# Where the edge network's second product of layer 2 is made: in the cluster pass of layer 1, or per node tile inside the MLP

## The chip, the cores and the metric

The kernel runs on one core of one Trainium2 chip. The metric is the device time of one launch in microseconds (us), here the median of three runs. A change of this kernel within about 0.2% (6.5 us) can't be told from no change.

## The reference, cut to what matters

Four graph layers run one after the other on 3,750 nodes with 256 features and 63,750 edges. Each adds its result to x. The change touches only how layer 2's edge term is made:

```python
# layer 1 (cluster layer), cut
logits = gcn_conv(h, W)          # 256 -> 10, summed over neighbours with a normalised adjacency
x = x + h + softmax(logits) @ cluster_emb
...
# layer 2, cut
e   = relu(ea @ ee_w1 + ee_b1) @ ee_w2 + ee_b2      # per edge: 64 -> 256 -> 256
agg = segment_sum(h[src] + e, dst)
h   = (1 + eps) * h + agg
h   = relu(ln(h @ w1 + b1)); h = relu(ln(h @ w2 + b2)); y = h @ w3 + b3    # the MLP, 256 -> 1024 -> 1024 -> 256
x   = x + relu(ln(h_in + y))
```

The sum over edges and the product with `ee_w2` can be exchanged, so the kernel sums the hidden rows `relu(ea @ ee_w1 + ee_b1)` per node during layer 0's edge loop, and multiplies by `ee_w2` once per node. With deg the number of edges of a node, the edge term is `HS^T @ ee_w2 + deg * ee_b2`.

## The kernel before, in words

There are NT = 30 node tiles of P = 128 nodes, taken as NJ = 15 pairs in the MLP. Five engines run programs of their own, written out by hand in the order in which they run, and synchronised by counting semaphores; there is no scheduler. `SUMS` holds five rows of 3,880 node columns: `HS` is rows 3 and 4 (the hidden sums, 256 features by nodes), `AG` rows 1 and 2, `DEG` row 0. `EW2` is `ee_w2`. `PS` is PSUM, eight banks of 512 float32.

The stages that matter here, in order:

- The **cluster pass** of layer 1 (TensorE L1072 to L1108). The adjacency matrix lies in DRAM as bfloat16 (`a_d`), and SyncE loads it tile by tile (`adjacency`) in column groups of 1,024: groups 0 to 3 have 30 tiles of 256 KB each, group 4 has 30 tiles of 166 columns. There are NR = 7 buffers; a tile can be loaded only when the tile seven places before it was used (`a_used`). For each wide tile TensorE makes two matmuls (L1088, 30 x 512). In groups 0 and 1 it also spreads the degree row to all partitions in eight matmuls (`spread_counts`, L1068, one after every seventh tile), each copied out by ScalarE (L689). VectorE writes 24 one-hot blocks (`first_one_hot`, L1589, from L1714) and then, in `cluster_sums`, copies each group's sums out of PSUM (L1671, L1673) and sends `d_free`. TensorE's group g from 2 on waits for `d_free` of group g-2.
- Softmax and the turned rows of layer 2. VectorE then adds `DEG * ee_b2` to `AG` in two instructions (L1763), and `neighbours` adds the neighbour sums.
- The **MLP** (TensorE from L1138, loop `dense_pair`). A pair is tiles i = 0 and 1. The order in TensorE's program for pair j is: dense1(1,j), dense2(0,j) first half, turn_hidden(1,j,0), dense2(0,j) second half and dense2(1,j) first half, turn_hidden(0,j,1), edge_part(0,j+1), dense2(1,j) second half, dense1(0,j+1), dense3(0,j), turn_hidden(1,j,1), edge_part(1,j+1), turn_hidden(0,j+1,0), dense3(1,j). All dense products are L1153, the turns L822, edge_part L1145. `edge_part` makes four products of 128 x 128 into the tile's PSUM bank, and VectorE's `dense_in` (L1783) adds them to `AG` and writes `HIN`, the input of dense1.
- VectorE per layer and tile: `hidden_stats` (L1790 to L1795, then the two scalars L1777 and L1778); per tile `dense_out` (from L1803). It writes the tile's output out of the PSUM banks that turn_hidden(i,j+1,0) needs next: that turn waits for `m_out`. ScalarE: `hidden_norm` (L723, L725) and `hidden_relu` (L736), of which dense3 waits for the last of eight.

A float32 matmul is shown in the trace as two records. So edge_part's four products are eight records, dense3's eight are sixteen.

## Time and profile before

| | us |
|---|---|
| median of 3 runs | 3268.11 |
| lowest, highest | 3263.8, 3269.29 |
| profiled execution: span on the page | 3494.0 |
| its own device time | not given, so the span stands for it |

| stretch of the profiled execution, us from its start | what runs |
|---|---|
| to 1777 | layer 0 and its edge loop, scatters of the adjacency |
| 1817 to 1927 | cluster pass |
| 1927 to 2330 | softmax, neighbour sums of layer 2 |
| 2330 to 3087 | MLP |
| 3087 to 3494 | layer 3 |

The profiled execution is 226 us longer than the median of the timed runs. Which of its stages are stretched the page can't tell; the change works in two stages and its effect is counted as a difference there, in us, and put on the median.

How to read it: "busy" is the time in which an engine executes; the number in brackets at a row's end is how long the engine sat idle before that row, and what it waited for. Matmuls are pipelined, so the distance from one row's start to the next one's is what a row costs, not its duration.

### The profile page before, as it was taken

The numbers are of one execution on the slowest core, as the hardware profiler recorded it, in microseconds if no ns is written. First come the engines' busy times: TensorE is split into PE (matmuls) and PEld (weight loads), VectorE is DVE, ScalarE is ACT, GpSimd is POOL, SyncE is SP. The second block draws the span as 40 slices with busy tenths as digits, with TensorE's granted clock in tenths as the row PEclk, the third lists the DMA queues.
The fourth block names the chain that finished last, engine by engine and source line by source line (L and its number), as shares of the span: only waits on it lengthen the run. The fifth ranks groups of instructions, "written<-read, shape, count | busy, mean of one in ns | idle before, by whom it ended". The sixth has DMA issues, their size and how long they took to land.

```text
span 3494.0 us, 48240 instructions
## 1 busy us (share of the span) xinstructions
PE 2934.6 (84%) x15020; PEld 1947.6 (56%) x15084; DVE 1869.1 (53%) x5320; ACT 1260.7 (36%) x3665; POOL 1013.3 (29%) x1048
## 2 busy tenths in 40 slices
PE   2799936888888888889268799989999999999998
PEld 2444416777777777778142444445555555545545
DVE  6578745666666665556250543334555555532334
ACT  1122235666666666668020220004444444420000
POOL 2144465666666666665710000000000000000000
PEclk6699968898999899999559699999999999999999
DMA  8966643222222222221128243330000000022232
GB/s 250 363 180 194 183 125 86 70 73 74 71 74 71 73 74 72 74 66 28 31 71 301 82 119 103 101 118 6 3 6 6 6 3 6 23 76 79 78 101 80
DMA packets 245032, 314.35 MB, mean 90 GB/s; under 512 B 121467, under 2 KB 168484, under 8 KB 240740
## 3 DMA queue, kind: packets, MB, share of 16 engines
q1 hardware_dynamic: 191412, 175.79, 17.8%
q0 software_dynamic: 49104, 104.11, 10.2%
q10 hardware_dynamic: 4320, 31.95, 2.3%
q8 instruction: 109, 1.79, 0.2%
q14 instruction: 87, 0.71, 0.1%
HBM read 234.14 MB, written 77.59 MB: 89 GB/s over the span
## 4 chain that ended last, share of the span: by engine, by line
PE 57%; DVE 15%; issue 11%; ACT 7%; another core or an unknown queue 4%; DVEq 3%; DMA 3%; SPq 0%; ACTq 0%
PE PS L1153 15%; PE PS L998 14%; PE PS L964 7%; PE PS L939 5%; PE PS L977 5%; PE PS L822 4%; ACT BG L653 3%; DMA BG<-a_d 3%; DVE BG L1703 2%; DVEq L1582 2%; DVE OHB L1430 1%; ACT SL L736 1%; DVE AL L1790 1%; DVE SUMS L1411 1%
## 5 line engine op out<-in xcount | busy, mean ns | idle before, releaser
L1567 DVE TENSOR_TENSOR SUMS<-SUMS,PS 128x640 f32 x500 | 409.2, 818 | 374.2 <-PE PS L939 220.7
L532 POOL DMA_INDIRECT BG<-feat_d,IDXST x500 | 485.9, 972 | 337.9 <-PE PS L939 157.4
L523 POOL DMA_INDIRECT a_d<-VAL,IDXS x499 | 492.3, 987 | 314.3 <-DVE VAL L1424 133.2
L1153 PE MATMUL PS<-BG,SL 128*128 128x512 f32 (+1 forms) x1440 | 539.1, 530 | 12.0 <-ACT SL L736 12.0
L653 ACT ACTIVATE BG<-BG,SL 128x64 f32<-128x64 f32 x2000 | 513.4, 336 | 0.0
L1153 PEld LDWEIGHTS PS<-BG,SL 128*128 128x128 f32 x1440 | 277.0, 195 | 251.7 <-issue 222.4
L564 POOL MEMSET BG<- 128x7680 f32 x1 | 6.5, 6501 | 1327.3 <-DVE MV L1834 1327.3
L964 PE MATMUL PS<-W1A,X 65*128 65x256 f32 x1000 | 295.2, 421 | 81.8 <-ACT X L627 60.4
L939 PE MATMUL PS<-OHB,BG 128*128 128x128 f32 x2000 | 357.2, 305 | 0.2
L977 PE MATMUL PS<-OHB,X 128*128 128x128 f32 x2000 | 337.5, 295 | 23.1 <-issue 22.6
L977 PEld LDWEIGHTS PS<-OHB,X 128*128 128x128 f32 x2000 | 306.7, 208 | 40.0 <-issue 25.1
L939 PEld LDWEIGHTS PS<-OHB,BG 128*128 128x128 f32 x2000 | 287.3, 207 | 1.8
L822 PE MATMUL PS<-IDENT,X 128*128 128x128 f32 (+3 forms) x700 | 167.6, 282 | 103.2 <-issue 80.3
L964 PEld LDWEIGHTS PS<-W1A,X 65*128 65x128 f32 x1000 | 184.8, 206 | 118.2 <-ACT X L627 74.3
L634 ACT ACTIVATE X<-PS 128x512 f32<-128x512 f32 x250 | 148.7, 595 | 264.2 <-PE PS L964 128.5
L871 PE MATMUL PS<-SUMS,BG 128*128 128x512 f32 x480 | 241.9, 635 | 0.0
L723 ACT ACTIVATE SM<-SM,EPSC 128x1 f32<-128x1 f32 x60 | 17.7, 294 | 539.9 <-DVE SM L1795 539.9
L998 PE MATMUL PS<-AL,BG 128*128 128x512 bf16 (+1 forms) x906 | 192.2, 368 | 4.5 <-DVE SUMS L1758 3.0
L998 PE MATMUL PS<-AL,SUMS 128*128 128x512 bf16 (+1 forms) x893 | 187.3, 364 | 5.2 <-DVE X L1906 3.0
L736 ACT ACTIVATE SL<-PS,COL 128x128 f32<-128x128 f32 x480 | 173.7, 475 | 26.0 <-PE PS L822 25.9
L1703 DVE TENSOR_TENSOR SUMS<-SUMS,OHB 128x2 f32 x499 | 81.6, 163 | 159.1 <-issue 93.0
L599 ACT ACTIVATE SUMS<-PS 128x512 f32<-128x512 f32 x120 | 71.6, 597 | 259.9 <-PE PS L871 219.2
(298 smaller groups left out, 4093.0 us busy)
## 6 DMA issues: line engine op xcount, KB each, us to landing
BG<-a_d SPq DMA_DIRECT2D x171, 256.0 KB, 4.2
AL<-a_d SPq DMA_DIRECT2D x137, 256.0 KB, 2.6
a_d<-BG POOLq DMA_DIRECT2D x30, 1088.0 KB, 40.2
feat_d<-SUMS ACTq DMA_DIRECT2D x30, 1040.0 KB
BG<-rel_d SPq DMA_DIRECT2D x100, 160.0 KB
X<-in_edge_attr_dram SPq DMA_DIRECT2D x124, 128.0 KB
SUMS<-a_d SPq DMA_DIRECT2D x52, 256.0 KB, 2.6
SL<-key_d SPq DMA_DIRECT2D x50, 192.0 KB
```

The lines of the kernel that those rows point to most:

```text
L523: pool.indirect_dma_start(a_d.rearrange("n (w o) -> (n w) o", o=1), bass.IndirectOffsetOnAxis(ap=IDXS[:, t:t + 1], axis=0), VAL[:, t:t + 1 ...
L532: pool.indirect_dma_start(RING[:, t // NB % 3, t % NB, :], None, feat_d.rearrange("n (r d) -> (n r) d", r=R), bass.IndirectOffsetOnAxis(ap ...
L653: last = act.activation(m, m, ACT.Copy, scale=EXT[:, b % 2, k, 1 + q:2 + q])
L736: last = act.activation(H1T[:, i, c, :], PS[:, 4 + 2 * i + c // 4, (c % 4) * P:(c % 4 + 1) * P], ACT.Relu, scale=COL8[:, 2 * l, c:c + 1], ...
L822: return pe.transpose(out_ap, in_ap, IDENT[0:k, 0:k])
L871: last = pe.matmul(PS[:, 4 + q, :], HT[:, c, t * P:(t + 1) * P], WALL[:, c, q * 512:(q + 1) * 512], start=(c == 0), stop=(c == 1))
L939: last = pe.matmul(at[:, (c + 1) * P:(c + 2) * P], RING[:, b % 3, k, c * P:(c + 1) * P], OH[:, k % 10, :], start=True, stop=True)
L964: last = pe.matmul(EDGE_HIDDEN[:, k * D:(k + 1) * D], EAT[v % 2][:, 2 * q + k, :], W1A[:, :], start=True, stop=True)
L977: pe.matmul(SUM_AT[n % 3][:, (3 + c) * P:(4 + c) * P], HM[v % 2][:, k, c * P:(c + 1) * P], OH[:, n % 10, :], start=True, stop=True)
L998: last = pe.matmul(PS[:, 4 * (g % 2) + 2 * c + o // 512, 0:m], lhs(t, part)[:, c * P:(c + 1) * P], rhs[:, o:o + m], start=(t == 0 and part ...
L1153: last = pe.matmul(PS[:, to + q, 0:width], lhs[:, i, c, :], w[:, c, q * width:(q + 1) * width], start=(c == 0), stop=(c == kc - 1))
L1567: add = tt(a, a, SUM_AT[n % 3].rearrange("p (a n) -> p a n", a=5), ALU.add)
```

## The change

The `ee_w2` products of all 30 tiles are made in groups 0 and 1 of the cluster pass. After the matmuls of an adjacency tile TensorE makes one `edge_part`, for the first time after tile 4 of group 0 and then 30 times up to tile 27 of group 1, into PSUM banks 6 and 7 in turn (waiting for `ee_home` of the tile two before). VectorE's new `edge_home` adds `DEG * ee_b2` and writes the result over `HS`, in two instructions per tile; it stands ahead of each one-hot block. VectorE starts `cluster_sums` only after all 30. `spread_counts` goes to banks 4 and 5 and stands after every third tile of group 0. Later one addition `AG += HS` takes the place of the two of L1763. In the MLP `edge_part` and its semaphores are gone, and `dense_in` is a copy of `AG` to `HIN`.

```diff
@@ ScalarE
-                act.activation(DEG[:, 512 * c:512 * c + n], PS[:, 4 + c % 4, 0:n], ACT.Copy).then_inc(s("deg_sb"), 1)
+                act.activation(DEG[:, 512 * c:512 * c + n], PS[:, 4 + c % 2, 0:n], ACT.Copy).then_inc(s("deg_sb"), 1)
@@ TensorE, cluster pass
-                if c >= 4:
-                    pe.wait_ge(s("deg_sb"), c - 3)
+                if c >= 2:
+                    pe.wait_ge(s("deg_sb"), c - 1)
...
+            def edge_part(e):
+
+                if e >= 2:
+                    pe.wait_ge(s("ee_home"), e - 1)
+                for f in range(2):
+                    for c in range(2):
+                        last = pe.matmul(PS[:, 6 + e % 2, f * P:(f + 1) * P], EW2[:, c, f * P:(f + 1) * P],
+                                         HS[:, c, e * P:(e + 1) * P], start=(c == 0), stop=(c == 1))
+                last.then_inc(s("ee_ps"), 1)
...
                 if g == 2:
                     pe.wait_ge(s("deg_sb"), 8)
+                    pe.wait_ge(s("ee_home"), NT)
...
-                    if g < 2 and t % 7 == 6:
-                        spread_counts(4 * g + t // 7)
+                    if g == 0 and t % 3 == 0 and t // 3 < 8:
+                        spread_counts(t // 3)
+                    if edges_home < NT and (g * NT + t - 4) * NT >= edges_home * 54:
+                        edge_part(edges_home)
+                        edges_home += 1
@@ TensorE, MLP
-            def edge_part(i, j):
-
-                for f in range(2):
-                    for c in range(2):
-                        last = pe.matmul(PS[:, 2 * i, f * P:(f + 1) * P], EW2[:, c, f * P:(f + 1) * P],
-                                         HS[:, c, bass.ds((2 * j + i) * P, P)], start=(c == 0), stop=(c == 1))
-                last.then_inc(s(f"m_ee{i}"), 1)
...
                 turn_hidden(0, j, 1)
-                if more:
-                    pe.wait_ge(s("m_var0"), 2 * j + 2)
-                    edge_part(0, j + 1)
                 dense2(1, j, 1)
...
                 if more:
-                    edge_part(1, j + 1)
                     turn_hidden(0, j + 1, 0)
                 dense3(1, j)
 
-            edge_part(0, 0)
-            edge_part(1, 0)
@@ VectorE
+            def edge_home(e):
+
+                dve.wait_ge(s("deg_sb"), e // 4 + 1)
+                dve.wait_ge(s("ee_ps"), e + 1)
+                for c in range(2):
+                    last = stt(out=HS[:, c, e * P:(e + 1) * P], in0=DEG[:, e * P:(e + 1) * P], scalar=B2C[:, c:c + 1],
+                               in1=PS[:, 6 + e % 2, c * P:(c + 1) * P], op0=ALU.mult, op1=ALU.add)
+                last.then_inc(s("ee_home"), 1)
...
-            for i in range(6 * LB):
-                last = first_one_hot(i // 6, i % 6)
-            step(last)
+            for e in range(NT):
+                edge_home(e)
+                if e < 6 * LB:
+                    last = first_one_hot(e // 6, e % 6)
+                if e == 6 * LB - 1:
+                    step(last)
+            dve.wait_ge(s("ee_home"), NT)
             cluster_sums()
...
-            for c in range(2):
-                step(stt(out=AG[:, c, 0:NPAD], in0=DEG[:, 0:NPAD], scalar=B2C[:, c:c + 1], in1=AG[:, c, 0:NPAD],
-                         op0=ALU.mult, op1=ALU.add))
+            step(tt(AG[:, :, 0:NPAD], AG[:, :, 0:NPAD], HS[:, :, 0:NPAD], ALU.add))
...
             def dense_in(i, j):
-                dve.wait_ge(s(f"m_ee{i}"), j + 1)
-                mine(dve, tt(HIN[:, i, :, :], AG[:, :, bass.ds((2 * j + i) * P, P)],
-                             PS[:, 2 * i, 0:D].rearrange("p (c n) -> p c n", c=2), ALU.add), f"m_hin{i}", j + 1)
+                mine(dve, cp(HIN[:, i, :, :], AG[:, :, bass.ds((2 * j + i) * P, P)]), f"m_hin{i}", j + 1)
```

TensorE in groups 0 and 1 of the cluster pass, before: L1088 is the adjacency product, L1068 the spread of the degrees. This is the start of group 0 and what follows it.

```order
4713 L1088 MATMUL PS<-BG 30x512 x14
4714 L1068 MATMUL PS<-SUMS,ONES 128x512
4715 L1088 MATMUL PS<-BG 30x512 x14
4716 L1068 MATMUL PS<-SUMS,ONES 128x512
4717 L1088 MATMUL PS<-BG 30x512 x14
```

The same place after, from tile 3 of group 0 on; L1099 is the adjacency product now, L1077 the four products of an edge_part.

```order
4716 L1068 MATMUL PS<-SUMS,ONES 128x512
4717 L1099 MATMUL PS<-BG 30x512 x2
4718 L1077 MATMUL PS<-SUMS,EW 128x128 x4
4719 L1099 MATMUL PS<-BG 30x512 x4
4720 L1068 MATMUL PS<-SUMS,ONES 128x512
4721 L1077 MATMUL PS<-SUMS,EW 128x128 x4
4722 L1099 MATMUL PS<-BG 30x512 x4
4723 L1077 MATMUL PS<-SUMS,EW 128x128 x4
```

Between two edge_parts stand one or two adjacency tiles (two or four matmuls) and nothing else but a spread.

TensorE in the MLP's loop, before, from the second turn (turn_hidden(0,j,1)) to the turn behind dense3(0,j):

```order
4850 L822 MATMUL PS<-IDENT,AL 128x128 x8
4851 L1145 ISA
4852 L1145 MATMUL PS<-SUMS,EW 128x128
4853 L1145 ISA
4854 L1145 MATMUL PS<-SUMS,EW 128x128 x3
4855 L1153 MATMUL PS<-BG,SL 128x512 x8
4856 L1158 REGISTER_ALU
4857 L1153 MATMUL PS<-BG,OHB 128x512 x4
4858 L1153 MATMUL PS<-BG,SL 128x256 x8
4859 L822 MATMUL PS<-IDENT,AL 128x128 x8
4860 L1145 ISA
```

and after, with the dense products at L1159, up to dense3(1,j):

```order
4905 L822 MATMUL PS<-IDENT,AL 128x128 x8
4906 L1159 MATMUL PS<-BG,SL 128x512 x8
4907 L1164 REGISTER_ALU
4908 L1159 MATMUL PS<-BG,OHB 128x512 x4
4909 L1159 MATMUL PS<-BG,SL 128x256 x8
4910 L822 MATMUL PS<-IDENT,AL 128x128 x8
4911 L1179 ISA
4912 L822 MATMUL PS<-IDENT,AL 128x128 x8
4913 L1159 MATMUL PS<-BG,SL 128x256 x8
```

The two turns at the end of a pair follow each other directly now. VectorE around the one-hot blocks (L1589), at the end of them and ahead of the first copy of `cluster_sums` (L1671 before, L1680 after), before and then after:

```order
2339 L1713 ISA
2340 L1589 SCALAR_TENSOR_TENSOR BG<-IOTA,QC,BG 125x640 x24
2341 L1671 COPY OHB<-PS 30x512
2342 L1673 COPY SUMS<-PS 30x512
```

```order
2386 L1670 SCALAR_TENSOR_TENSOR SUMS<-SUMS,COL,PS 128x128 x2
2387 L1589 SCALAR_TENSOR_TENSOR BG<-IOTA,QC,BG 125x640
2388 L1670 SCALAR_TENSOR_TENSOR SUMS<-SUMS,COL,PS 128x128 x12
2389 L1680 COPY OHB<-PS 30x512
2390 L1682 COPY SUMS<-PS 30x512
```

L1670 is edge_home; the copies of group 0's sums now stand behind the last of them.

## Rows read from the trace of the kernel before

**Rows 1.** The page: busy time of TensorE, and the chain by engine

```profile
PE 2934.6 (84%) x15020; PEld 1947.6 (56%) x15084; DVE 1869.1 (53%) x5320; ACT 1260.7 (36%) x3665; POOL 1013.3 (29%) x1048
PE 57%; DVE 15%; issue 11%; ACT 7%; another core or an unknown queue 4%; DVEq 3%; DMA 3%; SPq 0%; ACTq 0%
```

**Rows 2.** Busy time by stretch: groups 0, 1, 2 with 3

```profile
core 0: us, PE busy (x) PEld busy (x) DVE busy (x) ACT busy (x) POOL busy (x), PEclk, DMA share, GB/s
1817.20:1842.00 24.80, 22.25 (x68) 5.92 (x68) 18.91 (x24) 2.39 (x4) 0.00 (x0) 0.85 0.94 320
1842.00:1866.50 24.50, 21.16 (x74) 5.46 (x72) 1.79 (x3) 3.18 (x5) 0.00 (x0) 1.00 0.98 343
1866.50:1914.20 47.70, 38.61 (x254) 11.23 (x254) 3.65 (x9) 0.31 (x1) 0.00 (x0) 1.00 0.91 313
```

**Rows 3.** TensorE in order of time, groups 0 and 1: start us, duration us

```profile
1817.25 1.87 PE L1088 MATMUL PS<-BG 128*30 128x512 bf16 x4 [3.82 <-DMA BG<-a_d]
...
1825.45 3.19 PE L1088 MATMUL PS<-BG 128*30 128x512 bf16 x14
1828.57 1.12 PE L1068 MATMUL PS<-SUMS,ONES 1*128 1x512 f32 x2
1829.62 1.04 PE L1088 MATMUL PS<-BG 128*30 128x512 bf16 x4
...
1865.96 0.62 PE L822 MATMUL PS<-IDENT,OHB 30*125 30x30 f32 x4
```

**Rows 4.** VectorE in time there; then a tile of SUMS (ns min/median/max)

```profile
1816.92 19.19 DVE L1589 SCALAR_TENSOR_TENSOR BG<-IOTA,QC,BG 125x640 bf16<-125x640 f32 x24
1842.47 0.68 DVE L1671 COPY OHB<-PS 30x512 f32<-30x512 f32 x1 [6.36 <-PE PS L1088]
...
L1758 DVE TENSOR_SCALAR SUMS<-PS,COL x60: 399/402/410, 1981.2 to 2057.6; 128x128 f32<-128x128 f32 x60
```

**Rows 5.** TensorE in order of time, one pair of the MLP

```profile
2502.18 1.05 PE L822 MATMUL PS<-IDENT,AL 128*128 128x128 f32 x8
...
2517.68 1.06 PE L1145 MATMUL PS<-SUMS,EW 128*128 x8
2518.58 7.03 PE L1153 MATMUL PS<-BG,SL 128*128 128x512 f32 x16
2525.45 3.60 PE L1153 MATMUL PS<-BG,OHB 128*128 128x512 f32 x8
...
2533.21 1.06 PE L1145 MATMUL PS<-SUMS,EW 128*128 x8
2535.61 1.06 PE L822 MATMUL PS<-IDENT,AL 128*128 128x128 f32 x8 [1.35 <-DVE BG L1803]
2537.30 3.72 PE L1153 MATMUL PS<-BG,SL 128*128 128x256 f32 x16 [0.63 <-ACT SL L736]
...
2551.16 1.05 PE L822 MATMUL PS<-IDENT,AL 128*128 128x128 f32 x8
```

**Rows 6.** VectorE and ScalarE in order of time, the same pair

```profile
2525.65 1.23 DVE L1790 TENSOR_TENSOR AL<-PS,BG 128x1024 f32<-128x1024 f32 x1 [5.37 <-PE PS L1153]
...
2533.03 0.16 DVE L1778 SCALAR_TENSOR_TENSOR SM<-SM 128x1 f32<-128x1 f32 x1
2534.49 0.42 DVE L1783 TENSOR_TENSOR OHB<-SUMS,PS 128x256 f32<-128x256 f32 x1 [1.30 <-PE PS L1145]
...
2533.23 1.24 ACT L725 ACTIVATE AL<-AL,SM 128x1024 f32<-128x1024 f32 x1 [0.49 <-DVE SM L1778]
2534.38 2.88 ACT L736 ACTIVATE SL<-PS,COL 128x128 f32<-128x128 f32 x8
```

**Rows 7.** A dense3(1,j) at the lower clock: TensorE in time, and by stretch

```profile
2684.23 5.41 PE L1153 MATMUL PS<-BG,SL 128*128 128x256 f32 x16 [0.64 <-ACT SL L736]
...
2685.00:2687.50 2.50, 2.50 (x8) 1.96 (x7) 1.54 (x4) 2.15 (x7) 0.00 (x0) 0.50 0.00 0
```

**Rows 8.** TensorE in order of time, the first instructions of the MLP

```profile
2330.37 2.02 PE L1145 MATMUL PS<-SUMS,EW 128*128 128x128 f32 x16 [0.74 <-DVEq L1696]
2332.23 3.60 PE L1153 MATMUL PS<-BG,OHB 128*128 128x512 f32 x8
```

More of the change, by code:

```diff
@@ L1063, in spread_counts @@
             def spread_counts(c):
-                if c >= 4:
-                    pe.wait_ge(s("deg_sb"), c - 3)
+                if c >= 2:
+                    pe.wait_ge(s("deg_sb"), c - 1)
                 n = min(512, AW - 512 * c)
-                pe.matmul(PS[:, 4 + c % 4, 0:n], ONES[0:1, :], SUMS[0:1, 0, 512 * c:512 * c + n],
+                pe.matmul(PS[:, 4 + c % 2, 0:n], ONES[0:1, :], SUMS[0:1, 0, 512 * c:512 * c + n],
                           start=True, stop=True).then_inc(s("deg_ps"), 1)
+            def edge_part(e):
[6 more added lines that the diff above has]
+                last.then_inc(s("ee_ps"), 1)
             def cluster_turn(t):
@@ L1074, in _ @@
             pe.wait_ge(s("ys_ready"), 1)
-            turned = 0
+            turned = edges_home = 0
             for g, (c0, w) in enumerate(GROUPS):
```

## The prediction

> **What bounds the kernel now.** TensorE is busy for most of the span and heads the chain [rows 1], but a share says nothing of the two stages that the change touches, so I read each by itself: first the stretches, then the order of time on TensorE, then on the engines that it waits for.
>
> In the cluster pass the transfers set the pace. Their share is 0.94 and 0.98 in groups 0 and 1, at 320 and 343 GB/s [rows 2], and TensorE waits again and again for a tile of the adjacency. Its own need there is less than its busy time looks. Where it isn't waiting, 14 matmuls go from 1825.45 to 1828.57 [rows 3], 0.223 us each, so the 120 of both groups need 26.8 us. A spread takes 1.05 us (1828.57 to 1829.62), eight about 8.2. The first five us run at the lower clock (the granted mean of group 0 is 0.85 [rows 2], that is about 7 of 24.8 us at half of full speed, of which TensorE sat waiting for part), which costs about 2.5. Together 37.5 us. The two groups take 48.7 (1817.25 to 1865.96). So TensorE has some 11 us to spare, no more.
>
> In the MLP TensorE sets the pace, with two waits in each pair of tiles: 1.35 us ahead of turn_hidden(0,j+1,0), for VectorE's output addition L1803, and 0.63 ahead of dense3(1,j), for ScalarE's L736 [rows 5]. A pair takes 48.98 us (2502.18 to 2551.16), and there are 15.
>
> **The change part by part.** *Products added to the cluster pass.* An edge_part costs 0.90 us (2517.68 to 2518.58 [rows 5]) at the full clock. Thirty are 27.0 us; between matmuls of another shape a little more of a weight load may show, so I take 0.95, 28.5 us. 37.5 + 28.5 = 66.0 us of TensorE against 48.7 now: **17.3 us** later at the end of group 1, and TensorE has become the bound there. The bounds are 27.0 us with nothing lost between shapes (+15.8) and 31 (+19.8), if an edge_part costs 0.13 more or TensorE waits now and then for ee_home. VectorE keeps up, but only just: two instructions like L1758, 0.40 us each [rows 4] (the nearest row: 128x128, out of PSUM, with a pointer scalar), and a one-hot of 19.19 / 24 = 0.80 make 1.6 us per tile, against 1.8 adjacency tiles of 0.45 and one edge_part, 1.75 us, on TensorE. Two banks take up the jitter.
>
> *The added wait.* VectorE copies group 0's sums only after the last edge_home, and TensorE's group 2 waits for that copy. Behind edge_part 29 TensorE has two tiles left, 0.9 us. VectorE needs 0.8 for edge_home, 0.68 for L1671 [rows 4] and the same for L1673, and about 0.2 between them: 2.4. So TensorE stands 1.5 us: **+1.5**, nothing at best. Queued behind that wait is all of group 2, and SyncE's transfers behind it, since no buffer comes free.
>
> *What the slower groups give back.* While TensorE is the bound, transfers run ahead until all seven buffers are full. Groups 2 and 3 are still bound by transfers: 60 tiles in 47.7 us [rows 2], 0.795 each. They start with up to seven tiles in hand, worth at most 5.6 us; the transfers must start again behind the wait, which takes some 2 us of it away. I take **-4**, between -5.6 and -2. The cluster pass in all: 17.3 + 1.5 - 4 = **+14.8**, from 10 to 19.
>
> *Spread of the degrees.* The same eight matmuls, earlier; counted above. ScalarE copies each in time, three tiles before the bank is needed again. Zero.
>
> *The two additions L1763.* One addition of 7,680 elements in place of two of 3,840: the same VectorE work within a few tenths, and TensorE is in the neighbour sums meanwhile, which wait for nothing here. Zero; if the cover were gone, a few tenths.
>
> *Products taken out of the MLP.* 28 edge_parts of 0.90 us stand in 14 of the pairs, 25.2 us. Whether both of a pair count is to be read from the waits. edge_part(0,j+1), at 2517.68, stands ahead of dense2(1,j)'s second half with no wait near: it goes in full, 0.90 us. Everything after follows from the end of that dense2, T = 2525.45 [rows 5]. VectorE starts its statistics at T + 0.20 and works through two tiles' of them without a pause to L1778, done at T + 7.74 [rows 6]; ScalarE's L725 runs on from T + 7.78, and only then the eight L736 of tile 1, from T + 8.93 to T + 11.81; dense3(1,j) starts at T + 11.85 (2537.30). In none of this does edge_part(1,j+1) stand, which ran at T + 7.76 in TensorE's spare time. So it saves **nothing**: the wait grows. Turn_hidden(0,j+1,0) comes earlier, because dense_in (which waited 1.30 us for the products, 2534.49 [rows 6]) is a copy that starts at once: L1803 ends near T + 8.7 and not at T + 10.0. But dense3(1,j) still starts at T + 11.85. TensorE's waits in a pair become about 0.9 + 1.95 = 2.9 us in place of 1.98. From dense3(1,j) on the chain is the same as now. So 14 x 0.90 = **-12.6**. The first pair has its two products on the way from VectorE's last sum to dense1: 1.86 us (2330.37 to 2332.23 [rows 8]) become a copy of some 0.4 and its semaphores: **-1.2**. In all -13.8.
>
> *The clock.* In 5 of the 14 pairs the granted clock fell to 0.50, the lower level of 1.2 GHz, just after these two waits, and dense3(1,j) took 5.41 us in place of 3.72 [rows 7]: 1.7 us each, 8.5 us in all. What TensorE did before each fall was always the same 1.98 us of waits with eight transposes between. With 2.9 us of waits in the same place I expect more falls, 9 to 11 of 14, each at 1.5 us on average (part of some falls will lie in the waits): 15 us against 8.5, **+7**; bounds -2 (even fewer falls than now, three or four) and +12 (all 14). The Trainium skill ("TensorE: Matmul & The Clock Gate", "Why this matters for your kernels") puts the fall down to idle gaps between bursts that are longer than any wait in this loop; by it there would be no falls here, before or after. The trace disagrees: 5 falls with no wait above 1.35 us.
>
> Sum: 14.8 - 13.8 + 7 = **+8**, to 3268.1 + 8 = **3276 us**. On the profiled execution it would be 3494 + 8 = 3502. That one is 226 us longer than the median; nothing in the two stages shows a stretch, so I take the difference over as it is.
>
> **The rivals.** (A) The forecast, **3276** (3270 to 3284). Chance 0.48.
>
> (B) All as above, but the falls of the clock stay about as frequent, since they come and go with the phase of something that TensorE's program doesn't set: 9 of the 14 turns with the very same 1.98 us had none. (By the rule of the clock page cited above, waits of this size change nothing either, which is this case.) +1, **3269** (3265 to 3273). Chance 0.22.
>
> (C) The products hide under the transfers: TensorE waits for tiles in groups 0 and 1 and its weight loads (PEld) fill only 5.92 and 5.46 us of 24.8 and 24.5 [rows 2]. Even with all 27.0 us of the products added that is 38 of 49 us, below the stage's length. The cluster pass then costs at most 3 us: 3 - 13.8 + 7 = -4, **3264** (3258 to 3268). Against it: the streaming time of 0.223 us a matmul. It decides if the two groups end less than 5 us later. The Trainium skill ("Perfetto Trace Analysis", "Identifying the Most-Contended Engine") judges TensorE's room by just this share of weight loads, not by matmul busy time. Chance 0.10.
>
> (D) Both products of a pair are won, as a TensorE that waits only 2 us of 49 would suggest: 14.8 - 25.2 - 1.2, and with no waits added no more falls: -12, **3256**. It would need dense3(1,j) to start less than T + 11.85; the rows of VectorE and ScalarE leave no room for that. Chance 0.07.
>
> (E) The ending on the dear side: VectorE, not TensorE, paces the 30 edge_parts. If edge_home with its waits costs 1.1 us and not 0.8, a tile costs VectorE 1.9 to 2.0 us against 1.75, over the 24 that have a one-hot beside them: 4 to 6 us more, and TensorE's pauses may lower the clock there as well. 8 + 8, **3284** and above, to 3292. It decides once VectorE's step per tile is over 1.75 us in group 1. Chance 0.13.
>
> That the change doesn't do what it says is excluded by the order of instructions.
>
> **How the numbers follow.** Slower by over 0.2% (above 3274.6, which is about what a measurement can tell from no change): most of A (0.40) and all of E, 0.53. Within 0.2%: the rest of A, B, half of C, 0.35. Faster by over 0.2% (below 3261.6): D and the low end of C, 0.12. The range leaves out D and the far ends of C and E: 3260 to 3289.
>
> **What would show it.** The first transposes of group 2 (1865.96 now) should come 17 to 20 us after their distance from the pass's first matmul now, with TensorE hardly waiting for transfers in group 1 and once for VectorE's copy ahead of group 2; groups 2 and 3 should be about 4 us shorter. A pair of the MLP without a fall should take 48.1 us, with a wait near 0.9 ahead of the turn and one near 1.9 ahead of dense3(1,j). Count the 16-matmul rows of 5.3 us: 9 to 11, not 5. The prediction is wrong if a pair takes 47.2 us, if groups 0 and 1 end less than 10 us later, or if the falls don't grow in number.

## The result, and where the time went

The changed kernel takes **3277.75 us** (median of 12 runs, 3271.55 to 3282.35) against 3267.34 us for the kernel before on the same chip (12 runs, 3262.23 to 3272.02): a ratio of **1.0034**, 95% interval 1.0025 to 1.0043, slower by 8 to 14 us. The forecast was 3276 us.

The profiled execution of after has a span of 3270.5 us; that of before had 3494.0. To compare like with like I profiled the kernel before once more on the experiments' chip (run e0_before, span 3260.6). Stage by stage, in us:

| kernel | first adjacency matmul at | groups 0 and 1 | groups 2 and 3 | MLP | after the MLP |
|---|---|---|---|---|---|
| before, rows above | 1817.25 | 48.7 | 48.2 | 754.6 | 407.2 |
| before, profiled anew | 1589.17 | 47.3 | 46.6 | 751.8 | 407.3 |
| after | 1578.92 | 76.9 | 45.9 | 741.0 | 408.0 |

The MLP is counted from dense1(0,0) to the first transposes behind the last pair. The cluster pass pays 28 to 30 us more in its first half and gets 1 to 2 back; the MLP gives 11 to 14.

The page of after, busy time and the chain (against [rows 1]):

```profile
PE 2855.6 (87%) x15020; PEld 1896.9 (58%) x15084; DVE 1881.0 (58%) x5379; ACT 1255.7 (38%) x3665; POOL 1017.8 (31%) x1048
...
PE 49%; DVE 23%; issue 9%; ACT 6%; POOL 5%; DMA 4%; DVEq 3%; SPq 0%; POOLq 0%
```

TensorE has the same 15020 instructions; the page can't show that they moved. The stretches can. Groups 0 and 1 run from 1578.92 to 1655.80, groups 2 and 3 behind them (against [rows 2]; the columns are the same):

```profile
1578.92:1586.00 7.08, 7.08 (x12) 1.83 (x12) 0.00 (x0) 0.60 (x1) 0.00 (x0) 0.50 0.84 288
1586.00:1590.00 4.00, 4.00 (x13) 2.14 (x13) 0.32 (x2) 0.60 (x1) 0.00 (x0) 0.50 0.44 135
1590.00:1592.00 2.00, 2.00 (x7) 0.52 (x5) 1.09 (x3) 0.00 (x0) 0.00 (x0) 0.88 0.21 42
1592.00:1655.80 63.80, 62.59 (x349) 37.14 (x348) 37.27 (x84) 4.68 (x7) 0.00 (x0) 1.00 0.71 219
1655.80:1701.00 45.20, 38.11 (x248) 11.35 (x248) 3.45 (x8) 0.00 (x0) 0.00 (x0) 1.00 0.91 322
```

Two things are to be seen. TensorE is busy for 62.59 of 63.80 us while the DMA share falls from 0.94 and 0.98 to 0.71: the bound has passed from the transfers to TensorE, as forecast. And the granted clock stands at 0.50, the lower level, for 11.6 us at the start. TensorE's waits in the pass say the same: between the wait ahead of its first matmul and the one ahead of group 2 there is none. The whole list for groups 0 and 1 (engine, line, releaser: us in all, times, longest):

```profile
PE PS L1099 <- DMA BG<-a_d: 77.7, 1, 77.7
```

TensorE in order of time, the start of the pass, a stretch of its middle, and its end (against [rows 3]; L1077 are the products, L1068 the spreads, L1099 the adjacency tiles, two matmuls each):

```profile
1578.92 1.01 PE L1099 MATMUL PS<-BG 128*30 128x512 bf16 x2 [77.72 <-DMA BG<-a_d]
1579.86 2.07 PE L1068 MATMUL PS<-SUMS,ONES 1*128 1x512 f32 x2
...
1590.93 1.12 PE L1068 MATMUL PS<-SUMS,ONES 1*128 1x512 f32 x2
...
1616.77 1.16 PE L1077 MATMUL PS<-SUMS,EW 128*128 128x128 f32 x8
1617.86 1.04 PE L1099 MATMUL PS<-BG 128*30 128x512 bf16 x4
1618.83 1.16 PE L1077 MATMUL PS<-SUMS,EW 128*128 128x128 f32 x8
...
1622.94 1.16 PE L1077 MATMUL PS<-SUMS,EW 128*128 128x128 f32 x8
1624.03 0.61 PE L1099 MATMUL PS<-BG 128*30 128x512 bf16 x2
1624.56 1.16 PE L1077 MATMUL PS<-SUMS,EW 128*128 128x128 f32 x8
...
1653.55 1.04 PE L1099 MATMUL PS<-BG 128*30 128x512 bf16 x4
1655.82 0.40 PE L822 MATMUL PS<-IDENT,OHB 30*125 30x30 f32 x2 [1.23 <-DVE SUMS L1682]
```

A product with two tiles behind it takes 2.06 us (1616.77 to 1618.83), a product with one tile 1.62 (1622.94 to 1624.56). So a tile costs 0.44, as forecast (0.45), and a product 2.06 - 0.88 = **1.18 us**, not 0.95. A spread takes 2.07 us at the low clock and 1.12 at the full one.

VectorE in the same stretch (against [rows 4]; L1670 is edge_home, two instructions, L1589 the one-hot):

```profile
1618.04 0.61 DVE L1670 SCALAR_TENSOR_TENSOR SUMS<-SUMS,COL,PS 128x128 f32<-128x128 f32 x2 [0.65 <-PE PS L1077]
1618.56 0.88 DVE L1589 SCALAR_TENSOR_TENSOR BG<-IOTA,QC,BG 125x640 bf16<-125x640 f32 x1
1620.09 0.61 DVE L1670 SCALAR_TENSOR_TENSOR SUMS<-SUMS,COL,PS 128x128 f32<-128x128 f32 x2 [0.65 <-PE PS L1077]
```

It waits 0.65 us for TensorE in a step with two tiles, and still 0.22 in one with a single tile. VectorE is not what paces the products.

One pair of the MLP without a fall of the clock, and one with it (against [rows 5, 7]; L1159 with 16 matmuls of 256 columns is dense3(1,j)):

```profile
2174.37 1.09 PE L822 MATMUL PS<-IDENT,AL 128*128 128x128 f32 x8 [1.14 <-ACT AL L725]
2177.15 5.41 PE L1159 MATMUL PS<-BG,SL 128*128 128x256 f32 x16 [1.69 <-ACT SL L736]
...
2272.73 1.09 PE L822 MATMUL PS<-IDENT,AL 128*128 128x128 f32 x8 [1.29 <-ACT AL L725]
2275.51 3.72 PE L1159 MATMUL PS<-BG,SL 128*128 128x256 f32 x16 [1.69 <-ACT SL L736]
...
2320.92 1.09 PE L822 MATMUL PS<-IDENT,AL 128*128 128x128 f32 x8 [1.28 <-ACT AL L725]
2323.70 3.72 PE L1159 MATMUL PS<-BG,SL 128*128 128x256 f32 x16 [1.69 <-ACT SL L736]
```

The pair takes 48.19 us (2275.51 to 2323.70), 0.79 less than 48.98. Of the 14 pairs with a next one, **four** show a dense3(1,j) of 5.41 us, every fourth (2177.15, 2371.89, 2566.30, 2760.72); before had five, before profiled anew three. The forecast had said 9 to 11.

### The profile page after: what moved, and what is told of

Its sections match the earlier page's. It is cut to its first block, busy times and chain, and to the rows that moved or that the text cites. A ratio compares the mean times of both kernels' runs of the same rounds, so it can differ in the third digit from the quotient of the medians.

```text
span 3270.5 us, 48271 instructions
## 1 busy us (share of the span) xinstructions
PE 2855.6 (87%) x15020; PEld 1896.9 (58%) x15084; DVE 1881.0 (58%) x5379; ACT 1255.7 (38%) x3665; POOL 1017.8 (31%) x1048
## 4 chain that ended last, share of the span: by engine, by line
PE 49%; DVE 23%; issue 9%; ACT 6%; POOL 5%; DMA 4%; DVEq 3%; SPq 0%; POOLq 0%
PE PS L1159 16%; PE PS L998 15%; DVE SUMS L1567 4%; POOL a_d L523 3%; PE PS L822 3%; PE PS L939 3%; PE PS L964 3%; PE PS L977 2%; ACT BG L653 2%; POOL BG L532 2%; DVE BG L1712 2%; DVEq L1582 2%; DMA BG<-a_d 2%; DVE OHB L1430 2%; DVE X L1573 2%
## 5 line engine op out<-in xcount | busy, mean ns | idle before, releaser
L523 POOL DMA_INDIRECT a_d<-VAL,IDXS x499 | 490.3, 982 | 282.9 <-issue 134.4
L1159 PE MATMUL PS<-BG,SL 128*128 128x512 f32 (+1 forms) x1440 | 538.1, 530 | 26.6 <-ACT SL L736 26.6
L1159 PEld LDWEIGHTS PS<-BG,SL 128*128 128x128 f32 x1440 | 277.0, 195 | 265.3 <-issue 221.9
L939 PE MATMUL PS<-OHB,BG 128*128 128x128 f32 x2000 | 337.6, 293 | 0.0
L977 PE MATMUL PS<-OHB,X 128*128 128x128 f32 x2000 | 318.2, 283 | 1.7 <-DVEq L1545 1.7
L977 PEld LDWEIGHTS PS<-OHB,X 128*128 128x128 f32 x2000 | 288.2, 196 | 14.1 <-issue 1.7
L964 PE MATMUL PS<-W1A,X 65*128 65x256 f32 x1000 | 274.5, 398 | 3.2 <-ACT X L627 0.9
L939 PEld LDWEIGHTS PS<-OHB,BG 128*128 128x128 f32 x2000 | 269.7, 196 | 0.6
L964 PEld LDWEIGHTS PS<-W1A,X 65*128 65x128 f32 x1000 | 174.9, 195 | 26.6 <-ACT X L627 6.5
```

Source lines behind the costliest of these rows:

```text
L523: pool.indirect_dma_start(a_d.rearrange("n (w o) -> (n w) o", o=1), bass.IndirectOffsetOnAxis(ap=IDXS[:, t:t + 1], axis=0), VAL[:, t:t + 1 ...
L939: last = pe.matmul(at[:, (c + 1) * P:(c + 2) * P], RING[:, b % 3, k, c * P:(c + 1) * P], OH[:, k % 10, :], start=True, stop=True)
L964: last = pe.matmul(EDGE_HIDDEN[:, k * D:(k + 1) * D], EAT[v % 2][:, 2 * q + k, :], W1A[:, :], start=True, stop=True)
L977: pe.matmul(SUM_AT[n % 3][:, (3 + c) * P:(4 + c) * P], HM[v % 2][:, k, c * P:(c + 1) * P], OH[:, n % 10, :], start=True, stop=True)
L1159: last = pe.matmul(PS[:, to + q, 0:width], lhs[:, i, c, :], w[:, c, q * width:(q + 1) * width], start=(c == 0), stop=(c == kc - 1))
```

## The experiments

My theory after the result: the pass costs 28 us and not 15 because a product between tiles of another shape is dearer than one in the MLP and because the clock rises later; the product of tile 1 of each pair, taken out of the MLP, gives nothing, because it stood in TensorE's wait for VectorE and ScalarE; and the falls of the clock hang on something other than the length of the waits. The rivals: VectorE or the place of the products in the pass sets the price (E); both products are won in the MLP (D); the waits alone set the falls (the forecast's own step).

**e0_before** is the kernel before, unchanged.

> The kernel before, once more, for a second profile, since its first one was 226 us longer than the timed runs. If the first profile's two stages were not stretched: cluster pass 110 us from its first matmul to its last, a pair of the MLP 48.98 us without a fall of the clock, and 3 to 7 falls. If the stretch was in them too, the pass or the pair is shorter here. A wait of TensorE of some 75 us ahead of the cluster pass, as the kernel after shows it, should be here as well.

Measured: 3262.38 us in its one run; its stages are in the table above. What it adds is the start of the pass. TensorE there:

```profile
1589.17 1.86 PE L1088 MATMUL PS<-BG 128*30 128x512 bf16 x4 [76.92 <-DMA BG<-a_d]
1591.41 3.40 PE L1088 MATMUL PS<-BG 128*30 128x512 bf16 x8 [0.37 <-DMA BG<-a_d]
```

TensorE stands idle for **77 us** ahead of the pass, in before as in after (77.72). [Rows 3] show 3.82 us at this place: in that execution, 226 us longer than the median, TensorE's work ahead of the pass ended only at 1813.4, some 50 us behind the last scatter (1763.5), and the wait wasn't there to be seen. What ends it are the last scatters of the adjacency, issued by GpSimd one after the other (POOL L523, 1.26 us apart) up to 1566.44, and the transfers behind them. That is where work is free, and the next kernel puts it there.

**e1_in_hole**: all spreads and products ahead of the pass, in that wait.

```diff
             pe.wait_ge(s("ys_ready"), 1)
+            for c in range(8):
+                spread_counts(c)
+                for e in range(4 * c, min(4 * c + 4, NT)):
+                    edge_part(e)
...
-                    if g == 0 and t % 3 == 0 and t // 3 < 8:
-                        spread_counts(t // 3)
-                    if edges_home < NT and (g * NT + t - 4) * NT >= edges_home * 54:
-                        edge_part(edges_home)
-                        edges_home += 1
```

> The kernel after with all eight spreads and all 30 products made ahead of the cluster pass's first tile, in the time in which TensorE and VectorE wait for the last scatters of the adjacency (some 74 us). My theory: the products cost the pass 26 us only because TensorE has no more to spare there; in the wait they cost nothing, the pass is back at 108 to 111 us, the MLP keeps its 13.5 us: 3254 us, 4 per mille below before. Rival 1: products and one-hot blocks, bound by VectorE at 1.5 us each or run at the lower clock at 2.1 us each, take longer than the wait and push the pass back by up to 10 us: 3264. Rival 2: the MLP's gain came from elsewhere, 3267.

Measured: **3249.19 us** against 3265.38, ratio 0.9954 [0.9941, 0.9967]. It beats both kernels. Groups 0 and 1 take 44.4 us, groups 2 and 3 48.7, the MLP 740.9. TensorE in order of time:

```profile
1551.66 0.76 PE L1068 MATMUL PS<-SUMS,ONES 1*128 1x296 f32 x2
1552.35 2.05 PE L1077 MATMUL PS<-SUMS,EW 128*128 128x128 f32 x16
1584.20 7.07 PE L1103 MATMUL PS<-BG 128*30 128x512 bf16 x20 [29.80 <-DMA BG<-a_d]
1591.69 0.60 PE L1103 MATMUL PS<-BG 128*30 128x512 bf16 x2 [0.42 <-DMA BG<-a_d]
```

The products are done 29.80 us before the first tile arrives, and the transfers bound the pass again. So the 28 to 30 us of after come from the place of the products, not from the products themselves; and the MLP's gain of 11 us stands by itself.

**e2_spreads_ahead**: after, with only the eight spreads moved ahead of the pass (the two lines of spread_counts above out of the loop, a loop over c ahead of it).

> The kernel after with the eight spreads made ahead of the pass's first tile; the products stay where they are. My theory: groups 0 and 1 are bound by TensorE and each spread counts in full, 8.2 us at the full clock and 2 more for the two that ran at the lower one; the lower clock at the start also ends sooner, because the spreads (one row of the array each) were what kept it low for 11.6 us where before it was about 5. Groups 0 and 1 take 63 to 66 us against 76.9, the kernel 3266. Rival: the lower clock lasts as long without them, groups 0 and 1 take 67 to 69 us. Rival 2: the pass is bound by transfers after all and nothing moves.

Measured: 3266.78 against 3268.85, ratio 0.9992 [0.9979, 1.0006]. Groups 0 and 1 take 64.8 us in place of 76.9. The spreads themselves are 8.0 us of that (seven of 1.05, the last 0.69); the other 4 are the clock, which rises 3.5 us after the first tile in place of 11.6:

```profile
1584.37 4.08 PE L1101 MATMUL PS<-BG 128*30 128x512 bf16 x10 [57.83 <-DMA BG<-a_d]
1588.37 1.16 PE L1077 MATMUL PS<-SUMS,EW 128*128 128x128 f32 x8
```

The product at 1588.37 already takes 1.16 us, the full clock's time.

One profile each can't settle that the spreads keep the clock low. In e5, e6 and e9, which also have spreads among the first tiles, the clock rose 10.4, 11.6 and 11.1 us after the first tile; in e8, whose pass is that of after, it rose after 6.1, and groups 0 and 1 took 74.4 us. The second spread of e8 caught the rise (in after it took 2.07 us):

```profile
1590.54 1.36 PE L1068 MATMUL PS<-SUMS,ONES 1*128 1x512 f32 x2
```

The nine profiles without a spread behind one of the pass's first five tiles, e2 among them, show 3.2 to 7.3 us.

**e5_in_twos**: after, with two products at every second stop.

```diff
-                    if edges_home < NT and (g * NT + t - 4) * NT >= edges_home * 54:
-                        edge_part(edges_home)
-                        edges_home += 1
+                    if edges_home < NT and (g * NT + t - 6) * NT >= edges_home * 54:
+                        edge_part(edges_home)
+                        edge_part(edges_home + 1)
+                        edges_home += 2
```

> The kernel after with its products made in twos, 15 stops in place of 30, up to the same tile. My theory: an edge_part took 1.09 us and each stretch of adjacency matmuls about 0.08 more than without it, 0.26 us per stop over the 0.90 of the product alone, since the changes of shape are paid; half the stops save 15 times 0.26, groups 0 and 1 take 73 us. Rival: the product itself takes 1.09 us there, and they take 77 us. Against both: the second of the two waits for VectorE's edge_home, and it is slower.

Measured: 3270.57, ratio 1.0008 [0.9995, 1.0021]; groups 0 and 1 take 72.1 us. TensorE in time:

```profile
1614.90 2.05 PE L1077 MATMUL PS<-SUMS,EW 128*128 128x128 f32 x16
1616.89 1.47 PE L1099 MATMUL PS<-BG 128*30 128x512 bf16 x6
1618.28 2.05 PE L1077 MATMUL PS<-SUMS,EW 128*128 128x128 f32 x16
```

Two products and three tiles take 3.38 us (1614.90 to 1618.28); less three tiles of 0.44 that is 1.03 a product in place of 1.18. Thirty times 0.15 is 4.5 us, and the stage is 4.8 shorter. The price of a product in the pass depends on how often TensorE changes between products and tiles, which differ in shape and in type (float32 and bfloat16); which of the two differences costs, no run separates. That settles the first part of the theory as to the price; VectorE has the same work in e5 and after.

**e3_no_first** and **e4_no_second** take the product of one tile of each pair out of the kernel before and put it nowhere. e3 leaves out the product with `ee_w2` of tile 0 of each pair, e4 that of tile 1, so their results lack that term; dense_in then copies the rest of the sum.

```diff
 e3:
                     pe.wait_ge(s("m_var0"), 2 * j + 2)
-                    edge_part(0, j + 1)
 e4:
-                    edge_part(1, j + 1)
```

> The kernel before without the four products of tile 0 of each pair (edge_part(0,j)), which are left out of the computation; its dense_in is a copy. My theory: the whole 0.90 us of each goes, a pair takes 48.08 us, 12.6 us in 14 pairs plus about 1 at the start: 3254. Rival (both products of a pair count alike and the waits take half back): 48.5 us a pair, 3261.

> The kernel before without the four products of tile 1 of each pair (edge_part(1,j)), left out of the computation; its dense_in is a copy. My theory: they stand in a wait, so a pair still takes 48.98 us, the waits become 0.9 to 1.2 and 1.7 to 1.95 us, and the time is that of before within 2 us, but for the falls of the clock: if longer waits bring more falls, up to 12 us slower (9 to 11 falls); if the falls come by phase alone, 3 to 6 falls. Rival: 0.90 us less a pair, 3255.

Measured, e3: 3250.87 us, ratio 0.9959 [0.9944, 0.9974]; a pair takes 48.10 us, the MLP 737.5, two falls. Measured, e4: 3276.07 us, ratio **1.0031** [1.0022, 1.0041]: slower, with work left out. A pair without a fall takes 49.0 us, as in before (48.98), and ten of the 14 have a fall; the MLP takes 761.2. TensorE in e4:

```profile
2510.93 1.09 PE L822 MATMUL PS<-IDENT,AL 128*128 128x128 f32 x8 [1.16 <-ACT AL L725]
2513.71 5.41 PE L1153 MATMUL PS<-BG,SL 128*128 128x256 f32 x16 [1.69 <-ACT SL L736]
...
2561.59 1.09 PE L822 MATMUL PS<-IDENT,AL 128*128 128x128 f32 x8 [1.16 <-ACT AL L725]
2564.38 3.72 PE L1153 MATMUL PS<-BG,SL 128*128 128x256 f32 x16 [1.70 <-ACT SL L736]
```

So rival D falls: tile 0's product is worth 0.88 us a pair, tile 1's nothing; its time comes back as wait, 1.16 + 1.69 us in place of 1.35 + 0.63. And the step of the forecast that longer waits bring more falls holds here: ten, not three to five, at the same length of the pair. But after has waits as long, 1.27 + 1.69 us, and four falls.

**e6_filler** asks whether the waits matter at after's length of the pair: after, with four matmuls into an unused bank in the first wait.

```diff
                 if more:
+                    for f in range(2):
+                        for c in range(2):
+                            pe.matmul(PS[:, 2, f * P:(f + 1) * P], EW2[:, c, f * P:(f + 1) * P],
+                                      HS[:, c, 0:P], start=(c == 0), stop=(c == 1))
                     turn_hidden(0, j + 1, 0)
                 dense3(1, j)
```

> The kernel after with four products of tile 0 of HS, whose result nobody reads, put where edge_part(1,j+1) stood in the MLP, in TensorE's wait. A pair without a fall of the clock takes 48.2 us as in the kernel after; the wait ahead of the turn is 0.2 to 0.4 us in place of 1.27. If the length of the waits makes the falls: 0 to 2 of 14 in place of 4, up to 7 us faster. If they come by the pair's period alone: 4 again, and the time of the kernel after.

Measured: 3277.37 us, ratio 1.0032 [1.0017, 1.0047], the same as after. The waits shrink to 0.38 + 1.69 us, the pair stays at 48.18, and three pairs fall, every fourth:

```profile
2225.50 1.09 PE L822 MATMUL PS<-IDENT,AL 128*128 128x128 f32 x8 [0.61 <-ACT AL L725]
2228.28 5.41 PE L1159 MATMUL PS<-BG,SL 128*128 128x256 f32 x16 [1.69 <-ACT SL L736]
```

(In this early pair the first wait is still 0.61.) At this length of the pair 0.9 us of wait change nothing.

**e7_hole_filler** is e1 with the same filler, **e10_hole_half** the kernel before with the spreads and only tile 0's products moved ahead of the pass (VectorE copies them home there and dense_in adds them; tile 1's stay in the MLP, where e4 has shown them free), **e11_in_hole_again** is e1 once more beside them.

```diff
 e10, TensorE:
+            for c in range(8):
+                spread_counts(c)
+                for j in range(2 * c, min(2 * c + 2, NJ)):
+                    early_part(j)
...
                     pe.wait_ge(s("m_var0"), 2 * j + 2)
-                    edge_part(0, j + 1)
```

> Products and spreads ahead of the pass (as in e1_in_hole) and the filler of e6_filler in the MLP. If the filler takes falls away, 2 to 5 us below e1_in_hole, 3245; if not, the same 3249.

> All spreads and the products of tile 0 of each pair ahead of the pass; those of tile 1 stay in the MLP, in TensorE's wait. A pair takes 48.08 us against 48.18 in e1_in_hole, with waits of 0.64 and 1.35 at most, 2 to 4 falls: 1 to 4 us below e1_in_hole, 3247, if the waits and the tenth of a us count; the same 3249 if not.

> e1_in_hole once more, on the chip of e10_hole_half, to compare the two. 0.4 to 0.5% below before; a pass of 105 to 109 us and an MLP of 741.

Measured: e7 3249.96 us, ratio 0.9938 [0.9915, 0.9962]; e10 3246.38, 0.9948 [0.9935, 0.9962]; e11 3247.04, 0.9949 [0.9935, 0.9962]. The four kernels with the work in the wait can't be told apart. Neither a filler nor leaving the free product where it was brings anything that a measurement shows.

**e8_load_045** and **e9_load_090** lengthen the pair and leave the waits as they are: after, with two or four matmuls ahead of dense2(1,j)'s second half, where edge_part(0,j+1) used to stand.

```diff
                 turn_hidden(0, j, 1)
+                if more:
+                    pe.wait_ge(s("m_var0"), 2 * j + 2)
+                    for f in range(1):
+                        for c in range(2):
+                            pe.matmul(PS[:, 0, f * P:(f + 1) * P], EW2[:, c, f * P:(f + 1) * P],
+                                      IDENT[:, :], start=(c == 0), stop=(c == 1))
                 dense2(1, j, 1)
```

(e9 has `range(2)`.)

> The kernel after with two products of a constant, read by nobody, put back where edge_part(0,j+1) stood in the MLP, in the loaded stretch ahead of dense2(1,j)'s second half. The pair without a fall becomes 48.6 us, the waits stay 1.27 and 1.69. If the waits alone make the falls of the clock: 3 or 4 of 14, as in the four kernels with these waits at 48.18 us. If the pair's period counts as well: another number, not foretold.

> The same with four such products: a pair of 49.1 us with the waits of the kernel after, which is nearly e4_no_second (48.98 us, 10 falls). If period and waits together make the falls: 8 to 11 of 14. If something else of e4_no_second made its 10 falls: 3 or 4.

Measured, one run each: 3286.88 us (before: 3264.45) and 3298.36. The waits are 1.27 + 1.69 us in both, as in after. TensorE in e8:

```profile
2277.71 1.09 PE L822 MATMUL PS<-IDENT,AL 128*128 128x128 f32 x8 [1.29 <-ACT AL L725]
2280.50 5.41 PE L1159 MATMUL PS<-BG,SL 128*128 128x256 f32 x16 [1.70 <-ACT SL L736]
```

All pairs of all kernels together, the last one left out, which falls in every kernel:

| kernel | pair without a fall, us | the two waits, us | falls in 14 |
|---|---|---|---|
| before / profiled anew | 48.98 | 1.35 + 0.63 | 5 / 3 |
| e3 | 48.10 | 1.33 + 0.64 | 2 |
| e10 | 48.09 | 1.34 + 0.64 | 3 |
| after, e1, e2, e5, e11 | 48.18 | 1.27 + 1.69 | 4, 3, 3, 3, 4 |
| e6, e7 | 48.18 | 0.38 + 1.69 | 3, 4 |
| e8 | 48.64 | 1.27 + 1.69 | 7 |
| e9 | 49.08 | 1.27 + 1.69 | 8 |
| e4 | 49.0 | 1.16 + 1.69 | 10 |

With the waits held, the number of falls goes 3 to 4, 7, 8 (and 10 in e4) as the pair goes from 48.18 over 48.64 to about 49 us. In e8 and e9 0.45 and 0.90 us a pair should have cost 6.3 and 12.6 us; the MLP grew by 11.3 and 21.3, the rest by falls (two of e9's cost 3 us each).

## Why the prediction was right, step by step

The time, the sign and the range held; two of the three large terms did not, and their errors nearly cancelled. That the time came within 2 us is luck: 7 us forecast for falls of the clock that didn't come stood in for part of the 11 to 14 us by which the pass was too cheap. Two of the forecast's own signs failed. Groups 0 and 1 ended 28 to 30 us later, not 17 to 20, and the falls did not grow in number, which the forecast names as a sign of being wrong.

**Products added to the cluster pass: too small.** Forecast +17.3 with the wait of 1.5 beside it, 67.5 us for groups 0 and 1; measured 76.9. Term by term: tiles 0.44 us each, as forecast; spreads 8.0, as forecast (8.2). A product 1.18 us, not 0.95: 30 x 0.23 = 6.9 us, beyond even the upper bound (1.03). The step that failed is "between matmuls of another shape a little more of a weight load may show": the 0.05 us and the bound of 0.13 were read from no row. e5 shows that the added price goes with the changes between products and tiles; that it is a weight load isn't shown. The low clock: 11.6 us at half speed cost 5.8, where I had 2.5; the first two spreads now stand in its middle, and e2, without them, has the full clock after 3.5 (e8, with them, after 6.1). My five us were read from a pass that began with tiles alone. Together 26.7 + 8.0 + 35.4 + 5.8 + 1.2 = 77.1, against the 76.9 measured.

**The added wait: right.** 1.23 us, forecast 1.5. **Given back: too much.** Groups 2 and 3 took 45.9 us, 2.3 less than in the first profile of before (48.2) and 0.7 less than in before profiled anew; forecast 4, bounds 2 to 5.6. The pass in all is +26 to +29 us, not +14.8 (10 to 19).

**Products taken out of the MLP: right.** A pair takes 48.18 us, forecast 48.08; tile 1's product is free, as read from VectorE's and ScalarE's rows [rows 6], and e3 and e4 show it by themselves. The waits are 1.27 + 1.69 = 2.96 us, forecast 2.9, but divided otherwise and for another releaser: the turn now waits for ScalarE's L725. From VectorE's last sum to dense1 there are 0.91 us in place of 2.07, forecast -1.2. The whole term: 14 x 0.80 + 1.2 = 12.4, forecast 13.8. The 1.2 us lie ahead of dense1(0,0), and the stretch that holds them, from group 4 to dense1(0,0), did not get shorter: 419.8 us in after, 418.0 and 418.4 in before.

**The clock: wrong.** Forecast 9 to 11 falls and +7 us; measured 4 against 5 or 3, so nothing. The step that failed is "with 2.9 us of waits in the same place I expect more falls": it took the waits for the whole cause, and left out that the same change shortens the pair by 0.8 us. Each half is true alone. At 49.0 us longer waits bring ten falls (e4); at 48.18 they bring three or four, whether the first wait is 1.27 or 0.38 us (e6).

Rival B had the number of falls right, and its mechanism, "the phase of something that TensorE's program doesn't set", fits the traces. In each of the fourteen traces the moments at which the granted clock changes lie on one even raster of times, to within 0.01 us from the first change to the last, while the lengths of stages and pairs differ. Take where in a step of that raster dense3(1,j) starts, as a share of the step counted from a moment at which the clock can change. This sorts all 196 pairs without an exception:

| the two waits, us | pairs | falls | start of dense3(1,j) where the clock fell | where it did not |
|---|---|---|---|---|
| 1.35 + 0.63 (before, anew, e3, e10) | 56 | 13 | 0.836 to 1, 0 to 0.049 | 0.057 to 0.819 |
| 1.27 + 1.69, 1.16 + 1.69 (after, e1, e2, e4, e5, e8, e9, e11) | 112 | 42 | 0.832 to 1, 0 to 0.204 | 0.395 to 0.826 |
| 0.38 + 1.69 (e6, e7) | 28 | 7 | 0.843 to 0.921 | 0.455 to 0.807 |

The waits set how wide the part is in which a pair falls; the length of the pair sets at which places the pairs arrive. At 48.1 to 48.2 us each pair starts a little further on than the one before, falls once on entering that part and is thrown back to about the middle, so that the part's far end, and with it the wait, doesn't matter. At 49 us pairs also arrive at 0.057 to 0.162, where those of before did not fall and those of e4 did. No run moved the raster itself, and what keeps it is open.

The Trainium skill ("TensorE: Matmul & The Clock Gate", "Why this matters for your kernels") ties a fall to one idle gap longer than any in this loop. The traces disagree in every kernel: e4 has ten falls in its 14 pairs, and no wait above 1.70 us in them.

**What no step had.** The pass starts earlier in after. Before, VectorE makes the 24 one-hots at once, while GpSimd still issues scatters; after, it waits for products and makes them in the pass. GpSimd in order of time, in before profiled anew:

```profile
1515.84 0.96 POOL L523 DMA_INDIRECT a_d<-VAL,IDXS  x1 [0.30 <-issue]
1517.11 1.22 POOL L523 DMA_INDIRECT a_d<-VAL,IDXS  x1 [0.30 <-issue]
1518.63 1.29 POOL L523 DMA_INDIRECT a_d<-VAL,IDXS  x1 [0.30 <-issue]
...
1534.55 1.29 POOL L523 DMA_INDIRECT a_d<-VAL,IDXS  x1 [0.30 <-issue]
1536.14 0.96 POOL L523 DMA_INDIRECT a_d<-VAL,IDXS  x1 [0.30 <-issue]
```

VectorE in the same kernel, the row of the one-hots:

```profile
1515.82 19.19 DVE L1589 SCALAR_TENSOR_TENSOR BG<-IOTA,QC,BG 125x640 bf16<-125x640 f32 x24
```

And GpSimd in after, at the same time:

```profile
1518.65 0.96 POOL L523 DMA_INDIRECT a_d<-VAL,IDXS  x1 [0.30 <-issue]
...
1533.80 0.96 POOL L523 DMA_INDIRECT a_d<-VAL,IDXS  x1 [0.30 <-issue]
```

Twelve scatters take 1.29 us in place of 0.96 for just as long as the one-hots run: 3.9 us on the way to the pass. From the last gather to the first adjacency matmul there are 207.7 to 209.1 us in the three kernels with before's order (e0_before, e3, e4) and 205.1 to 206.5 in the six with after's (after, e2, e5, e6, e8, e9), about 3 less. So after gets some 3 us for nothing. No run was made for this alone, and the rest of the 10 us by which the table's starts differ is there at 460 us already, in code that is the same.

**The balance.** Against the first profile of before and the second: pass +26 and +29, start -3, from group 4 to the MLP +2 and +1, MLP -14 and -11, behind it +1: +12 and +17, against 8 to 14 measured. The stages are from one execution of each kernel, so the balance closes to some us and no better. The forecast had +14.8 and -6.8: the pass 11 to 14 too cheap, the MLP 4 to 7 too dear, the start 3 too late.

**The rivals.** C fell with the first stretch: groups 0 and 1 end 28 us later, not under 5. TensorE's weight loads filled only 11.4 of 49 us, and yet there was room for 11 us of work, not 38. The Trainium skill ("Perfetto Trace Analysis", "Identifying the Most-Contended Engine") would read TensorE's room from those loads, together with the share of its peak arithmetic that it does; here the spacing of matmuls that wait for nothing gave it, and even that only for matmuls of one shape. D fell by e4. E put the pass 8 us above the forecast, and it came 11 to 14 above; its mechanism isn't there: VectorE waits for TensorE in each step, by 0.22 to 0.65 us. That the change does what it says stands in the rows.

## What to carry to other kernels

Before moving work under a stage bound by transfers, look for the wait ahead of that stage: here thirty products were free in a 77 us wait and cost 28 to 30 us a few lines further down. Cost an instruction that is put between others of another shape by a row in which shapes alternate, and where there is none, take a bound of its own (here +30% over the same matmuls in a row). Work that stands inside a wait is not worth removing: it can even cost, since a longer wait may bring the lower clock.

## What the hardware showed that I had not expected

- The clock falls or not by the length of the loop as well as by the waits in it: with 1.27 + 1.69 us of waits, 4 falls in 14 at 48.18 us, 7 at 48.64, 8 at 49.08. They come at even distances (every sixth pair in e3 and e10, every fourth in after, every second in e8), and depend on where the waits land in a raster of times that runs on through the whole trace. In e8 and e9 a microsecond of work added to this loop cost 1.7 to 1.8.
- Leaving work out made a kernel slower (e4, 1.0031 [1.0022, 1.0041]).
- With spreads of one row each among the first tiles of the pass, the granted clock stayed at 0.50 for 10.4 to 11.6 us in four profiles, though TensorE didn't pause, and for 6.1 in a fifth (e8); in e2, without them, for 3.5. That the spreads are the cause is likely and not shown.
- Scatters issued by GpSimd are slowed by a third, 0.96 to 1.29 us, beside VectorE's one-hots, which read two operands from SBUF. The Trainium skill ("SBUF — State Buffer", "Who interferes with whom") says that such an instruction contends with GpSimd's reads, and infers that descriptor generation is spared. The trace shows the scatters held up, by 0.33 us each beside one-hots of 0.80; which part of a scatter waits it doesn't show.
- The profiled execution of before was 226 us longer than the timed ones and hid a wait of 77 us as 3.82. A profile so far from the median should be read as one of another case, above all at waits for another engine's queue.
